# Graph attention on one core: GpSimd's waits for TensorE's counts ahead of its gathers are replaced by three small memsets ahead of every fourth gather

## The reference

```python
# layer 0 (GAT)
h = (relu(layernorm(x)) @ W.T).reshape(N, 8, 16)
e = leaky(a_src[src] + a_dst[dst])            # per edge and head; loops added once more
p = exp(e - segment_max(e, dst)[dst])
x = x + segment_sum(p / segment_sum(p, dst)[dst] * h[src], dst) + bias
# layer 1 (transformer attention with edge bias)
score = (q[dst] * k[src]).sum(-1) / 4 + edge_attr @ We + be
p = exp(score - segment_max(score, dst)[dst])
msg = p / segment_sum(p, dst)[dst] * v[src]
x = x + layernorm(segment_sum(msg, dst) @ Wo + bo + x) * gamma + beta
```

## Time and profile before

| | us |
|---|---|
| median of 3 runs | 1561.81 |
| lowest, highest | 1560.83, 1562.72 |
| span of the profiled execution | 1585.9 |
| gathers of layer 0, first to last | 37.6 to 716.1 |
| gathers of layer 1, first to last | 799.2 to 1501.4 |
| busy: TensorE, VectorE, GpSimd, ScalarE | 1020.5, 934.6, 883.4, 640.0 |

### The profile page before, as it was taken

One profiled execution on the slowest core, in us unless ns is written; L12 is line 12 of the kernel. 1 busy time (PEld: TensorE's weight loads), 2 busy tenths in 40 slices (PEclk: granted clock), 3 DMA queues, 4 the chain that ended last, 5 costly groups with the idle time before them and its releaser, 6 DMA issues.

```text
span 1585.9 us, 21105 instructions
## 1 busy us (share of the span) xinstructions
PE 1020.5 (64%) x4985; PEld 863.7 (54%) x4985; DVE 934.6 (59%) x3002; ACT 640.0 (40%) x1699; POOL 883.4 (56%) x926
## 2 busy tenths in 40 slices
PE   5456666666665766666554577666766676676765
PEld 4345555555554555445354466565655566566664
DVE  6445656556565565557813455656565656656578
ACT  5524334243342433422554234444443434344414
POOL 5766666666666566551046566656666565666500
PEclk9655555555656565566766666877777777777676
DMA  6321222222222222222133222222222222232201
GB/s 138 72 66 43 66 46 66 48 63 45 67 47 67 45 65 47 58 84 57 49 94 95 73 84 84 84 80 80 84 84 84 80 82 81 84 88 83 80 1 41
DMA packets 54202, 110.35 MB, mean 70 GB/s; under 512 B 16876, under 2 KB 30848, under 8 KB 53956
## 3 DMA queue, kind: packets, MB, share of 16 engines
q0 software_dynamic: 36288, 91.12, 22.6%
q1 hardware_dynamic: 16483, 17.39, 4.0%
q10 hardware_dynamic: 1313, 0.50, 0.1%
HBM read 100.60 MB, written 8.81 MB: 69 GB/s over the span
## 4 chain that ended last, share of the span: by engine, by line
DVE 16%; PE 16%; another core or an unknown queue 10%; issue 9%; ACT 2%; DVEq 2%
PE bank L865 6%; PE bank L849 6%; DVE acc L1441 4%; DVE PV L1418 3%; DVE prod L1238 2%; PE bank L836 1%; PE bank L912 1%; DVE raw L1247 1%; DVE halves L1087 1%; PE bank L900 1%; DVEq L1441 1%; ACT S L636 1%; DVEq L1220 0%; DVEq L90 0%
## 5 line engine op out<-in xcount | busy, mean ns | idle before, releaser
L532 POOL DMA_INDIRECT G<-table,idx_all x880 | 857.1, 974 | 544.5 <-issue 280.3
L865 PE MATMUL bank<-PV,S 128*125 128x144 f32 x1760 | 449.5, 416 | 209.5 <-DVE acc L1441 104.4
L865 PEld LDWEIGHTS bank<-PV,S 128*125 128x125 f32 x1760 | 373.9, 287 | 236.1 <-issue 134.9
L1441 DVE TENSOR_TENSOR acc<-acc,bank 125x144 f32 x880 | 260.4, 296 | 339.3 <-remote 191.7
L636 ACT ACTIVATE S<-iota_n,lid 128x125 f32<-128x125 f32 x880 | 275.7, 386 | 0.7 <-issue 0.7
L849 PE MATMUL bank<-qe,ST 125*128 x880 | 182.0, 378 | 87.3 <-DVE prod L1238 80.7
L849 PEld LDWEIGHTS bank<-qe,ST 125*128 125x128 f32 x880 | 164.1, 279 | 96.7 <-issue 95.8
L1418 DVE TENSOR_TENSOR PV<-G,PV 128x512 f32<-128x512 f32 x220 | 151.2, 688 | 23.4 <-issue 22.8
L646 ACT ACTIVATE ST<-bank 125x512 f32<-125x512 f32 x110 | 63.6, 598 | 248.4 <-remote 197.6
L640 ACT ACTIVATE S<-S,ones 128x500 f32<-128x500 f32 x220 | 156.6, 712 | 7.3
L836 PE MATMUL bank<-ident,S 128*125 128x128 f32 x440 | 89.8, 340 | 52.5 <-ACT S L640 31.9
(11 more groups left out here) (219 smaller groups left out, 1093.8 us busy)
## 6 DMA issues: line engine op xcount, KB each, us to landing
G<-table,idx_all POOLq DMA_INDIRECT x880
prod<-in_edge_attr_dram SPq DMA_DIRECT2D x8, 672.0 KB
table<-G SPq DMA_DIRECT2D x12, 224.0 KB
bias_rows<-qe SPq DMA_DIRECT2D x1, 1664.0 KB
table<-h0b SPq DMA_DIRECT2D x8, 178.5 KB
out_dram<-G SPq DMA_DIRECT2D x8, 168.0 KB
prod<-in_edge_attr_dram SPq DMA_DIRECT2D x8, 90.0 KB
xs<-in_x_dram SPq DMA_DIRECT2D x1, 504.0 KB
```

The source lines that it names most:

```text
L532: pool.indirect_dma_start(G[:, u, v, 0:w], None, table, bass.IndirectOffsetOnAxis(ap=idx_all[:, g * GV + v:g * GV + v + 1], axis=0)).then_ ...
L865: last = pe.matmul(sums_bank(p)[0:BN, at:at + H * SLOT], S[:, ur, v, :], PV[:, v, :, :].rearrange("p h k -> p (h k)"), start=True, stop=True)
L1441: ve.tensor_tensor(a, a, o, ALU.add).then_inc(s.sem["acc_added"], 1)
```

## The change

`pace` and its calls are taken out, and with them every wait of GpSimd for `expanded`, `scoreT`, `hop1`, `hop2`, `t_done` and `mm_done`. The wait for `pv_ready` (and the one for `bias_transposed`) stays. Ahead of every fourth gather there are now three memsets of `w0n` (128x128 floats, zero), each of which waits for the count of the one before. The gather behind the third doesn't wait for it. That is 110 times three memsets in each layer. The other engines' instructions are the same in the same order.

```diff
-            def pace(n, g, v):
-
-                s, r, q = L[n], g - UNROLL, g - 1
-                if v % 4:
-                    return
...
-                if n == 0:
...
-                    if v == 8:
-                        wait(pool, s["scoreT"], g)
-                        if r >= 0:
-                            wait(pool, s["mm_done"], NB * r + 6)
...
-                else:
...
-                    if v == 8:
-                        wait(pool, s["hop2"], q)
-                        wait(pool, s["t_done"], 4 * q + 3)
-                        if r >= 0:
-                            wait(pool, s["mm_done"], NB * r + 3)
...
+            spaces = [0]
+
+            def space():
+
+                wait(pool, s_space, spaces[0])
+                pool.memset(w0n[:, :], 0.0).then_inc(s_space, 1)
+                spaces[0] += 1
...
                         for v in range(QV * j, QV * j + QV):
-                            pace(n, g, v)
+                            if v % 4 == 0:
+                                for _ in range(3):
+                                    space()
                             pool.indirect_dma_start(
```

More of the change, by code:

```diff
@@ L258, in gnn_kernel @@
         s_out = sem("out_written")
+        s_space = sem("spacer_set")
         s_bias3 = sem("bias_parts")
@@ L470, in _ @@
             pool.memset(acc[:, :, :], 0.0).then_inc(s_acc0, 1)
-            def pace(n, g, v):
-                s, r, q = L[n], g - UNROLL, g - 1
-                if v % 4:
-                    return
[L477 to L480, removed]
-                if n == 0:
-                    if v == 0:
-                        wait(pool, s["expanded"], 4 * q + 2)
-                        if r >= 0:
-                            wait(pool, s["mm_done"], NB * r + 3)
-                    if v == 4:
-                        wait(pool, s["expanded"], 4 * q + 4)
-                        if r >= 0:
-                            wait(pool, s["mm_done"], NB * r + 5)
-                    if v == 8:
-                        wait(pool, s["scoreT"], g)
-                        if r >= 0:
-                            wait(pool, s["mm_done"], NB * r + 6)
[L494 to L502, removed]
-                    if v == 8:
-                        wait(pool, s["expanded"], 4 * q + 3)
-                else:
[L506 to L510, removed]
-                        wait(pool, s["hop2"], q)
-                        wait(pool, s["t_done"], 4 * q + 3)
[L513 to L519, removed]
+            spaces = [0]
[3 more added lines that the diff above has]
+                spaces[0] += 1
             def gathers(n, table, w):
```

## The result

| | us | ratio to before, same chip |
|---|---|---|
| before | 1562.26 (1560.83 to 1564.03, 4 runs) | |
| changed | 1628.55 (1622.89 to 1639.69, 4 runs) | 1.0426, 95% 1.0379 to 1.0473 |

The change makes the kernel slower by 66 us, 4.3%. The forecast was 1490 us, and the direction was wrong. The time lies inside the range, on the side of rival 1. Ratios compare fast runs, those within 1.5% of their kernel's fastest, while the medians are of all runs; so a ratio can differ a little from that of the two medians beside it.

A forecast was written before the change was run, and what follows sets the result against it. GpSimd's gathers plus two pauses for late TensorE counts were taken to bound each group. Savings of 35 us in layer 0 and 11 and 26 us in layer 1, together 72, from 1561.8 gave 1490 us; range 1440 to 1800.

The forecast's parts named there:

- rival 1: Every group: space too short, TensorE's counts stay in, GpSimd runs to the ring's end; 1764 us, chance 0.25.
- What bounds the kernel before: Both loops: TensorE's counts don't come out during gathers, so GpSimd pauses about 2.4 us twice a group of 24.84 us.
- the 0.85 us for a triple: Time that three memsets add between gathers, taken as the middle of 0.5 and 1.2 us; four triples a group.
- is the new space long enough?: Behind each row of four gathers: whether TensorE's counts come out in about 1.15 us; judged yes, at 0.55.
- low end: Cheapest triple: starts 0.06 us behind the gather, next gather follows at once; adds 0.5 us, 22.0 us a group.
- high end: Dearest triple: 0.30 us gaps beside the gathers, memset steps of 0.34 us; adds 1.2 us, 24.8 us a group.
- the sum: Savings of 35 us in layer 0, 11 and 26 us in layer 1, together 72 us, giving 1490 us.
- the 1.35 us of the earlier trace: Layer 1 at 878.26: a VectorE wait ended 1.35 us after a row's last gather, cited for and against the space.
- Rival 2: Between gathers: a triple adds 1.3 us or more, losing what the change gained; 1545 to 1600 us, chance 0.10.
- rival 3: At the memsets: 660 more closely spaced GpSimd counts hold up TensorE's; time as with too short a space, chance 0.04.
- Rival 4: Mid group's chain on the other engines needs 24.8 and 25.6 us whatever GpSimd does; time stays, chance 0.06.
- The rule against the explanation: Skill's rule: DMAs never contend with compute, PE never waits; gathers then wouldn't delay TensorE, sum stays at 1490 us.

The follow-up runs named there:

- plain copies: Changed kernel without memsets, each gather replaced by a copy of 128 neighbouring rows: 1235.03 us, 0.7885 of before where counts come late; 1235.27 and 1234.32 us where prompt.
- the kernel with none: Changed kernel with the memsets taken out too, so no waits for counts: 1786.91 us, 1.1261 of before where counts come late; 1344.33 us, 0.9992 where prompt.

## Why the prediction was wrong, step by step

**What bounds the kernel before: right, for the kind of chip that it was timed on.** The two pauses of 2.4 us and the late counts were read rightly. The pauses are what late counts cost: on prompt chips a group takes 21.0 and 20.8 us in place of 24.84 and 25.58. The waits of `pace` keep the cost at that: with neither waits nor memsets the time is 1.126 of before. That all this depends on the chip I hadn't thought of. Whether it was the gathers or their transfers I had left unsaid; it is GpSimd's work on the gathers.

**The failed step: the 0.85 us for a triple, and with it the answer to "is the new space long enough?".** The triple adds 0.60 us, near the low end of 0.5. The space is 0.90 us, not 1.15, and 30 of 199 late counts came out in it. I took the middle "since neither end has a row with a gather beside a memset". The gaps of the high end are not there: the memset starts with the gather's end (0.00 us, not 0.30), the next gather starts 0.16 us behind the last memset (not 0.30), and the memsets go 0.27 us apart (not 0.34). A term that is a cost in one place and a length that must suffice in another shouldn't be set to its middle: cheap was the same as too short.

**"Is the new space long enough?" at the 1.15 us that I assumed: half right, and the sum was too large even so.** Four memsets give that space (1.17 us), and with it the kernel is a little faster than before (0.984). But 129 of 224 late counts still missed the space; the first length that let all of them out was 1.43 us. Layer 0 gives 24.2 us a group where I had 23.4, so (24.84 - 24.2) x 24.5 = 16 us in place of 35, and layer 1 gives 25.8, nothing in place of 26. Gathers that take up to 1.4 us (976 ns in the mean) cost about 0.5 us a group of that, and waits for the ring (48.9 us) are in the rest. 1490 us would have been wrong by the size too: 0.984 of 1561.8 is 1537.

**The number that was on the table.** I wrote that 1.15 is less than the 1.35 us of the earlier trace rows and that the other two freezes ended later, and still gave 0.55 to "long enough". Over the trace of before, half of the late counts that came out in a pause behind a row of eight came 1.6 to 1.9 us behind it. What helped 1.17 us is the length of the row, which I named only in passing: behind rows of four, in the kernel with six memsets, half came 1.0 to 1.1 us behind. At 0.90 us neither argument holds.

**Rival 1: the right mechanism, place and point of decision, with too high a price.** It said 1764 us. The kernel with no space at all is where that price belongs (1786.91, with 26.6 and 30.7 us a group); spaces of 0.90 us, in which 15% and 12% of the late counts come out, bring it to 1.043 and 1.079. Its chance of 0.25 should have been the larger one.

**Rival 2** (a triple costs more) and **rival 3** (the memsets' counts hold TensorE's) fell: 0.60 us, and nine memsets in a row go with a faster kernel, none with the slowest. The warning in the Trainium skill, VectorE: DVE Perf Modes, section The TRN2 errata, speaks of counts raised at a high rate by one engine that can bring another to a deadlock. Nothing of the kind shows here: with nine counts in 2.32 us all of TensorE's late ones came out in the space. **Rival 4** (the others set the pace) fell: with plain copies they need 1235 us.

**The rule against the explanation.** The plain copies make the same transfers on a late chip with no late count, which agrees with what the Trainium skill, SBUF — State Buffer, section Who interferes with whom, says of DMAs and compute engines. The other half, that PE never waits on anyone, agrees with the prompt chips (no late count of 1227). On the late ones (467 of 1077) TensorE's own work goes on, as the sums around 439 show, but its counts wait for GpSimd, and of counts that sentence says nothing. What was wrong was to read it as "GpSimd's gathers have no bearing on TensorE's results".

## What to carry to other kernels

A pause that lets something out has a length at which it works, and just below that it costs its own time and gives little: time it with one element more and one less before judging the idea. Waits that no data needs may be what keeps other engines alive; before removing them, ask what the engine will do in the time that it gains, and what stops it then. A pause that helps on one chip may be pure cost on the next, so a kernel tuned against such an effect has to be timed on more than one chip. The three kernels with memsets that gained on late chips weren't run on a prompt one; there the three kernels with memsets that were run lost 2 to 9%. The waits of the kernel before have the merit that they are long only where counts are late.

## What the runs showed of the hardware that was not expected

- Two kinds of chips under the same program: before takes 1562 to 1589 us in five sets of runs and 1342 and 1346 us in two, each set on one chip. Most gathers take the same 0.94 us on both. What differs is whether TensorE's counts come out while GpSimd works on indirect gathers. On a prompt chip the kernel with none has rows of up to 440 gathers and not one late count. Why chips differ in this stays open; no run could tell.
- The wait ends behind the row, later for longer rows: half of the late counts 1.0 to 1.1 us behind four gathers (six memsets), 1.6 to 1.9 behind eight (before), and 2.4 to 2.6 behind twelve (none). One such row of twelve, which ends at 426.30 with the sum out at 428.87:

```profile
425.36 0.94 POOL L491 DMA_INDIRECT G<-table,idx_all  x1 [0.30 <-issue]
430.70 0.95 POOL L491 DMA_INDIRECT G<-table,idx_all  x1 [4.40 <-DVE PV L1377]
```

```profile
428.87 0.30 DVE L1400 TENSOR_TENSOR acc<-acc,bank 125x144 f32 x1 [10.30 <-remote]
```

- Memsets between gathers are cheap to a fault: 0.27 us from one to the next with an awaited count, and 0.16 us from the last to the gather. The 0.30 us that stand between two gathers aren't added.
